# Expert units regrouped by token half, with the next attention's queries among them, in a two-layer cross-attention and mixture-of-experts kernel

## The reference

```python
x = x + L0_xattn(layernorm(x), ctx)     # 8 heads of 64
x = x + L0_ffn(layernorm(x))            # 8 experts, 2 chosen per token
x = x + L1_xattn(layernorm(x), ctx)     # 16 heads of 8, with biases
x = x + L1_ffn(layernorm(x))            # three layers of +-1 weights

# L0_ffn, for all tokens n and experts e:
logits = xf @ Wg
top_w, top_i = top_k(logits, 2); top_w = softmax(top_w)
combine = einsum('nk,nke->ne', top_w, one_hot(top_i, 8))
h = einsum('nc,ech->enh', xf, W1); g = einsum('nc,ech->enh', xf, W2)
y = einsum('enh,ehc->enc', silu(h) * g, W3)          # 256 hidden
out = einsum('enc,ne->nc', y, combine)
```

## Time and profile before

| | us |
|---|---|
| median of 3 runs | 237.65 (235.37 to 238.89) |
| the profiled execution | 236.75 |
| its span, first to last instruction | 234.0 |
| mean granted clock of TensorE | 0.992 of full |

### The profile page before, as it was taken

One profiled execution on the slowest core, in us unless ns is written; L12 is line 12 of the kernel. 1 busy time (PEld: TensorE's weight loads), 2 busy tenths in 40 slices (PEclk: granted clock), 3 DMA queues, 4 the chain that ended last, 5 costly groups with the idle time before them and its releaser, 6 DMA issues.

```text
span 234.0 us, 5028 instructions
## 1 busy us (share of the span) xinstructions
PE 223.9 (96%) x1825; PEld 186.7 (80%) x1825; DVE 167.4 (72%) x433; ACT 120.5 (51%) x288; POOL 69.9 (30%) x105
## 2 busy tenths in 40 slices
PE   8999998899999999999999999999799999989994
PEld 8778888798886889888988989777578887766783
DVE  1688757898887895465555548988668889598763
ACT  2566949689753742233223224355445656757642
POOL 5625599042500308813125700360000000220200
PEclk9999999999999999999999999999979999999999
DMA  6870001000000010201202270000000000000002
GB/s 171 222 196 5 1 3 46 3 0 0 3 0 3 0 49 22 67 22 46 67 0 67 71 202 22 4 0 0 3 0 3 3 0 3 0 3 1 0 0 90
DMA packets 11868, 8.18 MB, mean 35 GB/s; under 512 B 3012, under 2 KB 11144, under 8 KB 11848
## 3 DMA queue, kind: packets, MB, share of 16 engines
q1 hardware_dynamic: 11848, 7.91, 12.4%
HBM read 5.81 MB, written 0.52 MB: 27 GB/s over the span
## 4 chain that ended last, share of the span: by engine, by line
PE 81%; ACT 8%; DVE 8%; issue 1%; POOL 0%; DVEq 0%; ACTq 0%; POOLq 0%
PE ps L676 11%; PE ps L478 9%; PE ps L850 9%; PE ps L480 8%; PE ps L479 8%; ACT probs L983 6%; PE ps L795 4%; PE ps L767 4%; PE ps L754 3%; PE ps L474 3%; PE ps L566 3%; PE ps L485 2%; PE ps L555 2%; PE ps L780 2%; PE ps L469 2%; DVE probs L1308 2%
## 5 line engine op out<-in xcount | busy, mean ns | idle before, releaser
L1040 ACT ACTIVATE kT<-ps 128x512 f32<-128x512 f32 x32 | 19.1, 598 | 47.1 <-PE ps L480 47.1
L676 PEld LDWEIGHTS ps<-w,kT 128*128 128x128 f32 x256 | 30.9, 192 | 1.3
L676 PE MATMUL ps<-w,kT 128*128 128x128 f32 x256 | 31.0, 275 | 0.0
L1384 DVE TENSOR_TENSOR kT<-ps,kT 128x512 f32<-128x512 f32 x32 | 21.8, 689 | 11.0 <-PE ps L480 8.7
L1391 DVE SCALAR_TENSOR_TENSOR x_sb<-ps,comb,x_sb 128x128 f32<-128x128 f32 x64 | 18.0, 344 | 13.5 <-PE ps L676 13.5
L478 PE MATMUL ps<-xT_hi,w_hi 128*128 128x512 f32 x64 | 26.5, 414 | 0.2 <-DVE kT L1384 0.2
L480 PE MATMUL ps<-xT_hi,w_lo 128*128 128x512 f32 x64 | 25.2, 394 | 0.0
L479 PE MATMUL ps<-xT_lo,w_hi 128*128 128x512 f32 x64 | 25.0, 391 | 0.0
L983 ACT ACTIVATE probs<-ps,negmax 128x128 f32<-128x128 f32 x64 | 22.6, 410 | 1.8 <-DVE negmax L1296 1.8
L1478 DVE TENSOR_REDUCE probs<-ps 128x8 f32<-128x1024 f32 x16 | 19.4, 1224 | 4.5 <-PE ps L754 4.3
L415 POOL TENSOR_TENSOR w_hi<-w_raw,zero 128x512 fp32r<-128x512 f32 x8 | 9.3, 1163 | 42.9 <-DMA w_raw<-in_L_ffn_W 28.2
(11 more groups left out here) (208 smaller groups left out, 512.3 us busy)
## 6 DMA issues: line engine op xcount, KB each, us to landing
w_raw<-in_L_ffn_W SPq DMA_DIRECT2D x16, 128.0 KB, 2.2
k_st<-h_a SPq DMA_DIRECT2D x12, 128.0 KB, 2.7
w<-in_L_ffn_W SPq DMA_DIRECT2D x8, 128.0 KB, 2.2
x_sb<-in_x SPq DMA_DIRECT2D x2, 256.0 KB, 5.4
ctx_sb<-in_ctx SPq DMA_DIRECT2D x2, 192.0 KB, 3.3
w_raw<-in_L_xattn_Wq SPq DMA_DIRECT2D x1, 256.0 KB, 5.3
wo<-in_L_xattn_Wo SPq DMA_DIRECT2D x1, 256.0 KB, 4.9
k_i<-in_L_ffn_k SPq DMA_DIRECT2D x1, 256.0 KB, 3.3
```

The costliest lines, as they stand in the source:

```text
L676: ins = pe.matmul(ps[:, 4 + slot, k * C:(k + 1) * C], uT[:, slot, c, k * P:(k + 1) * P], w3[:, buf, c, :], start=(c == 0), stop=(c == NH - 1))
L1040: act.activation(silu[:, c, :], ps[:, c, :], ACT.Silu).then_inc(b_silu, 1)
L1384: dve.tensor_tensor(uT[:, slot, c, :], ps[:, 2 + c, :], silu[:, c, :], ALU.mult).then_inc(b_u, 1)
```

## The change

The units are taken from a table instead of loops. Half 0 is first done for all experts, from expert 2 on alone; then half 1 backwards. Experts 0 and 1 still do both halves in turn. Ten jobs (loads with their splits) serve sixteen units: experts 3 and 2 are loaded and split a second time for the last two units. There are four places for split weights and for W3 now: two as before, two in `h_a[:, 1]` and `wo0`. Splits 2 and 3 wait for `ln_lo` (the low part of the second half's input to the experts) in place of `b_g` and `a_wo`.

The first half's norm for the second attention is spread over units 10 to 13 (scaling now on ScalarE); the four query groups and their stacks lie among units 14 and 15. Behind the last unit the order of scores, maxima, fillers and the second half's norm is a new one, with 22 fillers in place of 25.

```diff
@@ constants
+        RAMP = (12, 3, 3, 2, 2)
+        JOBS = (0, 1, 2, 3, 4, 5, 6, 7, 3, 2)
+        SLOT = (0, 1, 2, 3, 0, 1, 2, 3, 3, 2)
+        UNITS = ((0, 0), (0, 1), (1, 0), (1, 1), (2, 0), (3, 0), (4, 0), (5, 0), (6, 0), (7, 0),
+                 (7, 1), (6, 1), (5, 1), (4, 1), (8, 1), (9, 1))
+        def done_before(j):
+            return max(q for q in range(NU) if UNITS[q][0] < j and SLOT[UNITS[q][0]] == SLOT[j]) + 1
+        def up_hi(j):
+            s = SLOT[j]
+            return w12_hi[:, s, :] if s < 2 else h_a[:, 1, 2 * (s - 2), :]
...
@@ sync
+            for j in (2, 3):
+                sp.wait_ge(b_lo, j - 1)
+                load_up(j)
+            sp.wait_ge(a_wo, NB)
+            for j in (2, 3):
+                load_down(j)
+            for j in range(4, len(JOBS)):
+                sp.wait_ge(b_lo, j - 1)
+                load_up(j)
+                sp.wait_ge(b_y, done_before(j))
+                load_down(j)
@@ gpsimd
+            def split_up(j):
+                pool.wait_ge(ld_up[j % 2], 32 * (j // 2 + 1))
+                if j >= 4:
+                    pool.wait_ge(b_g, NH * done_before(j))
...
-            pool.wait_ge(a_wo, NB)
-            for buf in range(2):
-                split_expert(2 + buf, buf)
+            pool.wait_ge(ln_lo, 2 * NT)
+            split_up(2)
+            split_up(3)
             pool.wait_ge(masks, 6)
             pool.tensor_copy(k_st[:, :, :].rearrange("p g n -> p (g n)"),
                              is_lo[:, 1:2].to_broadcast([P, NG * NB * P])).then_inc(k1_fill, 1)
+            split_up(4)
+            split_up(5)
...
@@ tensor
+            for q in range(NU - 2):
+                b_down(q)
+                b_hidden(q + 2, (0,))
+                if q + 2 == LAST[0] + 4:
+                    ln_transposes(2, 0)
+                if q + 2 == NU - 2:
+                    c_queries(0)
+                elif q + 2 == NU - 1:
+                    c_queries(2)
+                b_hidden(q + 2, (1,))
+                if q + 2 == NU - 2:
+                    c_queries(1)
+            b_down(NU - 2)
+            c_queries(3)
+            b_down(NU - 1)
             pe.wait_ge(k1_st, NK1)
-            keep_busy(6, M0)
             c_scores(0, 0)
             c_scores(0, 1)
-            keep_busy(5, M0)
+            keep_busy(RAMP[0], M0)
             c_scores(1, 0)
...
@@ vector
+            for q in range(NU - 2):
+                unit_add(q)
+                if q == LAST[0]:
+                    unit_stats(0)
+                if q == LAST[0] + 1:
+                    ln_refine(0)
+                    newton(dve.tensor_tensor(nm[:, 0:4], meanvar[:, 0:4, 0], rs[:, 0:4], ALU.mult))
+                    dve.tensor_scalar(nm[:, 0:4], nm[:, 0:4], -1.0, None, ALU.mult).then_inc(ln_nm, 1)
+                b_gate(q + 2, q % 2, (0,))
+                if q == LAST[0] + 2:
+                    ln_low(2, 0)
+                if q + 2 == NU - 2:
+                    c_query_stack(0)
+                b_gate(q + 2, q % 2, (1,))
...
```

More of the change, by code:

```diff
@@ L224, in program @@
         ld_up = [sem("ld_up0"), sem("ld_up1")]
-        ld_down = [sem("ld_down0"), sem("ld_down1")]
+        ld_down = [sem("ld_down" + str(i)) for i in range(4)]
         stored = sem("stored")
@@ L436, in _ @@
             pool.tensor_scalar(d2_w[:, :, :], k2_u[:, :, :], 2.0, -1.0, ALU.mult, ALU.add).then_inc(d_w, 1)
-            with pool.Fori(2, E // 2) as i:
-                for buf in range(2):
-                    split_expert(i * 2 + buf, buf)
+            split_up(6)
+            split_up(7)
             pool.memset(top_w, 0.0).then_inc(zeros_ok, 1)
@@ L1032, in _, with b_silu_step @@
             table(ACT.Silu)
-            def b_silu_step(q):
-                for c in range(NH):
+            def b_silu_step(q, chunks=range(NH)):
+                for c in chunks:
                     v = q * NH + c
@@ L1079, in c_query_signed @@
                                scale=sign[:, 0:1]).then_inc(c_part, 1)
-            ln_hi_copy(2, 0)
-            for n in range(NG):
-                c_query_signed(n)
+            for q in range(2, NU):
+                b_silu_step(q, (0,))
+                if q == LAST[0] + 4:
+                    ln_hi_copy(2, 0)
+                b_silu_step(q, (1,))
+                if q == LAST[0] + 3:
+                    ln_scale(2, 0)
+                if q == NU - 2:
+                    c_query_signed(0)
+                    c_query_signed(1)
+            c_query_signed(2)
+            table(ACT.Exp)
+            c_query_signed(3)
             def c_exp_half(b, a):
@@ L1140, in d_evacuate @@
                     d_whole(n)
-            act.wait_ge(ln_nm, 1)
-            for b in range(4, NB):
-                act.activation(xn[:, b, :], x_sb[:, b, :], ACT.Identity, bias=nm[:, b:b + 1],
-                               scale=rs[:, b:b + 1]).then_inc(ln_xn, 1)
+            ln_scale(2, 1)
+            c_exp_half(0, 0)
             ln_hi_copy(2, 1)
-            for s in range(NB + 1):
+            c_exp_half(0, 1)
+            c_query_signed(NG)
+            c_query_signed(NG + 1)
+            for s in range(1, NB + 1):
                 c_step(s)
@@ L1375, in _, with b_gate @@
             ln_low(1, 1)
-            def b_gate(q, slot):
-                for c in range(NH):
+            def b_gate(q, slot, chunks=range(NH)):
+                for c in chunks:
                     v = q * NH + c
@@ L1566, in _ @@
             c_top(0, 1)
+            c_shift(0)
             c_top(1, 0)
-            c_shift(0)
+            c_top(1, 1)
             ln_low(2, 1)
-            c_top(1, 1)
-            for s in range(NB + 2):
+            c_shift(1)
+            c_top(2, 0)
+            c_query_stack(NG)
+            c_top(2, 1)
+            c_query_stack(NG + 1)
+            for s in range(1, NB + 2):
                 c_step(s)
```

223 lines of the change are left out of this document (90 added, 133 removed).

## The result

| | before | after |
|---|---|---|
| median of 19 runs, us | 236.09 (234.84 to 238.89) | 237.71 (237.50 to 239.78) |
| the profiled execution, us | 236.75 | 237.69 |
| its span, us | 234.0 | 235.6 |

The ratio after to before is 1.0081, with a 95% interval of 1.0058 to 1.0103: slower by 0.8%, 1.6 us, and within the 2% that the prediction named. The forecast was +1.25 us. The forecast time of 238.9 was built on a median of three runs of before, 237.65; with more runs that median is 1.56 lower. The range held the time. Ratios leave out single executions that are over 1.5% slower than the fastest of the same kernel: a few of the kernel before, and two of the twelve of one variant, 255.8 and 256.2 us at a mean granted clock of 0.90, for which no run shows a cause.

The account below looks back on a forecast made before the run. TensorE was taken to bound the expert stage, VectorE's chain the boundary, VectorE's list also the gates. -3.0 + 3.4 + 0.85 = +1.25 takes 236.75 to 238.0; the median lies 0.9 higher: 238.9 us, range 234.0 to 241.0.

Parts of the forecast that it names:

- The fill blocks `gd`: At the gates, GpSimd's fill of `k_st` holds VectorE's `gd` until the fill ends, at 82.3; `gd` takes 2.5 to 3.5 us.
- Rival 1: At the gates, the fill does not block `gd`; no idle time or slow clock, the boundary's 3.0 stay: 234.6 us, chance 0.25.
- its rule: When VectorE and GpSimd instructions contend for their shared port, the later one waits until the earlier has ended, whatever its size.
- The loss at the gates: `b_hidden(3)` at 88.55 instead of 85.14, 3.4 us lost, plus 0.85 for a half-clock stretch after TensorE's wait before `b_hidden(2)`.
- Rival 2: At gates and experts, everything is caught and the clock falls where TensorE is full: +2.9, 240.6 us, chance 0.12.
- The boundary: From the last unit's end to `c_shifted(2,0)`: 4.2 + 21.2 = 25.4 us against 28.37, 3.0 us saved.
- the half clock: At the boundary, the old kernel's slow stretch from 168.8 to 172.2 goes away: 0.9 us of the 3.0 saved.
- the first 11.7: Behind the last unit, the time until the second half's low part is ready and query group 4 starts: 11.7 us.
- 9.45 of work without gaps: From 11.7 behind the last unit, TensorE's query, score, value and turn groups up to `c_shifted(2,0)`, with nothing late: 9.45 us.
- Rival 3: The boundary is not shortened: TensorE waits for maxima again or unit 12's gating is late; +3.25, 240.9 us, chance 0.13.
- The sum: Whole kernel: -3.0 + 3.4 + 0.85 = +1.25 us, from the profiled execution's 236.75 to 238.0.
- The fillers: Behind the last unit, 22 filler matmuls of 0.25 us, 5.5 us in all, run inside waits.

Follow-up runs that it names:

- the variant without contention: The changed kernel with GpSimd waiting, before splits 2 and 3, until the gates' weights are done: 234.25 us, ratio 0.9945 to the kernel before, span 231.9.

## Why the prediction was right, and where its terms were off

**The fill blocks `gd`: right.** Forecast 2.5 to 3.5 us, ending with the fill; measured 2.87. The fill reads one repeated column and holds VectorE all the same. Rival 1 is refuted by the two runs that move GpSimd away from it (0.15 and 0.16). The fill ended at 81.91 and not at 82.3: two of the three bias instructions were held by the splits, 1.27 and 1.25 for 0.34 and 0.50, but the splits hardly by them, and VectorE had slack there. One of the prediction's rows fits its rule only loosely: the product beside the cast lost 0.54 (1.77 for 1.23) where the cast had 0.86 left.

**The loss at the gates: right sign, 3.25 + 0.53 for 3.4 + 0.85.** `b_hidden(3)` would have come at 88.39 by VectorE's list and came at 88.92; forecast 88.55, then 0.85. Both terms were a little too large, together 0.47. The second thing caught was `gw`, not `pick`. Rival 2's fall of the clock where TensorE is full did not come here; two variants show it.

**The boundary: the mis-sized term, 2.17 for 3.0.** Of it 1.02 is the half clock (forecast 0.9), so the reordering itself is worth 1.15, not 2.1: the same 1.1 by which the variant without contention (231.9) lies under the undisturbed runs of before (233.0). Two places make the 0.83 (0.03 of it is rounding). The end of the last unit is pushed by 4.64 and not by 4.2: four transposes 0.47 (134.20 less 129.18, less the pace of 4.55), four query groups 1.87, 0.95 and 1.01, in sum 3.83 for 3.76, then 0.18 before the first scores, and 0.16 in units that take up to 4.59 each and not 4.55. Behind it `c_shifted(2,0)` comes at 21.56 and not 21.2: the first 11.7 were laid out rightly (11.68), but what I gave as 9.45 of work without gaps (its terms sum to 9.41) takes 9.88, with a wait of 0.18 and turns between kinds of matmuls. Laying work end to end with the shortest durations is a lower bound, and I used it as the value. Rival 3 needed 24 or more behind the first scores and did not come.

**The sum.** -2.17 + 3.25 + 0.53 = +1.61, forecast -3.0 + 3.4 + 0.85 = +1.25. The errors partly cancel: the loss was too large by 0.47, the gain by 0.83; that so little is left of them in the sum is luck. The base was the other error. The 2.75 around the span was 2.1 in the profiled execution after, and the profiled execution of before was one with the slow stretch; its undisturbed runs are 1.0 shorter. Set against those, the change costs 2.6 us of span, not 1.6. That the medians also differ by 1.6 is chance: the median of the kernel before lies between its two lengths.

**The fillers: right that they hide, wrong to leave them unpriced.** The prediction costed 22 of them at nothing and did not say what their absence would cost, 3.2 us for ten.

**Still open.** Of the runs of the changed kernel with a span of 235.4 to 235.7, six report a mean clock of 1.0 and seven of 0.990 to 0.993, at the same length. By the 0.53 above the first should be shorter. Both profiles caught show the slow stretch, so whether those six had it and did not record it isn't known.

## What to carry to other kernels

Before GpSimd's work is moved to a place where it has time, look at what VectorE does there: a list of tiny instructions on which TensorE waits can lose the length of each GpSimd instruction that it meets, whatever its own size. The remedy that worked is one wait that lets GpSimd start behind the list; cutting the long instruction up or reordering VectorE's list around it made the kernel slower, and making it write-only won back about a third of the loss in the profiled execution. And an idle time of TensorE is priced with what follows it: where a further wait followed, the half clock cost 0.53, where TensorE was full, 1.46 and 2.76.

## What the runs showed of the hardware that was not expected

- A memset of 3.51 us on GpSimd let a `tensor_tensor` with two SBUF inputs pass (0.15) and held a cast of 128x64 until its end (2.68).
- Eight pieces of a fill took 0.61 to 0.66 each, 4.58 in all, where the one long fill took 3.59. Beside them and the split behind them six small instructions took 3.1 us more in sum (4.1 for 1.0), more than `gd` lost to the long fill (2.7).
- The half clock behind a wait of TensorE of 1.30 us appeared in about half of the runs of one kernel, by their length (38 of 69 have a span of 234.0 or more and a mean clock below 0.994), behind the same wait in both profiles that show it, and by the same measure in none of ten runs in which the wait was filled. A wait of 1.42 ahead of `b_hidden(2)` in another variant was followed by full clock.
- Taking 2.5 us of matmuls that nobody reads out of a ramp with waits of 0.2 to 0.8 us made the following 8 us run at half clock, and the kernel 3.1 us slower.
